# Rings of PSUM banks and SBUF copies for the last thirty groups, without the unread matmuls

## The reference, cut to what matters

```python
offset = _conv(data_im, offset_w)                    # 3x3, 18 channels
mask = jax.nn.sigmoid(_conv(data_im, mask_w))        # 3x3, 9 channels
...
val = w00 * gather(y0i, x0i) + w01 * gather(y0i, x1i) + w10 * gather(y1i, x0i) + w11 * gather(y1i, x1i)
val = val * msk                                      # (B, C, 9 taps, H, W)
out = jnp.einsum('op,bphw->bohw', weight, col)       # (32 x 288) times columns
...
x = x + _L3_conv_ref(_gn(x), ...)
```

## Time and profile before

| what | value |
|---|---|
| median of 3 runs | 1318.24 us (1309.74, 1318.24, 1324.23) |
| the profiled execution | 1326.25 us, its span 1324.4 us |
| TensorE matmuls, weight loads | 748.0 us busy (56%), 335.9 us (25%) |
| VectorE, ScalarE, GpSimd | 667.9 us, 265.7 us, 658.5 us busy |
| mean granted TensorE clock | 0.743 |

### The profile page before, as it was taken

One profiled execution on the slowest core, in us unless ns is written; L12 is line 12 of the kernel. 1 busy time (PEld: TensorE's weight loads), 2 busy tenths in 40 slices (PEclk: granted clock), 3 DMA queues, 4 the chain that ended last, 5 costly groups with the idle time before them and its releaser, 6 DMA issues.

```text
span 1324.4 us, 8552 instructions
## 1 busy us (share of the span) xinstructions
PE 748.0 (56%) x2516; PEld 335.9 (25%) x2517; DVE 667.9 (50%) x913; ACT 265.7 (20%) x360; POOL 658.5 (50%) x619
## 2 busy tenths in 40 slices
PE   3448487777781146465656565500227546655798
PEld 1233132222130123232323223300103212312345
DVE  5988358999672177686777776421003101311230
ACT  1201575555140231121211111100001000100011
POOL 0000006775067736655666635777764757656610
PEclk9669797999795567877677777555657757856799
DMA  4000330000521101111111135211110211111100
GB/s 93 0 0 0 72 80 0 1 0 1 112 68 50 48 23 42 42 40 36 42 42 44 42 77 123 61 52 53 52 48 22 52 38 50 40 40 46 42 12 16
DMA packets 22376, 56.17 MB, mean 42 GB/s; under 512 B 10288, under 2 KB 10672, under 8 KB 21104
## 3 DMA queue, kind: packets, MB, share of 16 engines
q0 software_dynamic: 18432, 37.79, 10.6%
q1 hardware_dynamic: 3056, 15.45, 5.4%
q10 hardware_dynamic: 864, 2.64, 0.9%
HBM read 42.21 MB, written 5.24 MB: 36 GB/s over the span
## 4 chain that ended last, share of the span: by engine, by line
issue 25%; PE 23%; DVE 19%; another core or an unknown queue 15%; ACT 3%; POOL 1%; DMA 1%; DVEq 0%; ACTq 0%; POOLq 0%
PE PS L1389 10%; DVE scratch L1112 4%; PE PS L785 4%; DVE scratch L1038 3%; DVE scratch L1119 2%; PE PS L769 2%; DVE prodg L751 2%; DVE PS L1035 2%; DVE scratch L1043 1%; PE PS L1211 1%; PE PS L852 1%; PE PS L853 1%; PE PS L995 1%; PE PS L787 1%
## 5 line engine op out<-in xcount | busy, mean ns | idle before, releaser
L740 POOL DMA_INDIRECT got<-corner_table,idx_slot x486 | 479.2, 986 | 301.4 <-DVE prodg L751 155.3
L785 PE MATMUL PS<-colT,wt 128*32 128x128 f32 x512 | 93.4, 343 | 216.9 <-issue 163.5
L1389 PE MATMUL PS<-parts,selb 96*128 96x512 bf16 x600 | 168.0, 421 | 77.8 <-issue 76.2
L980 PE MATMUL PS<-parts,selb 96*128 96x512 bf16 (+1 forms) x256 | 87.3, 438 | 121.2 <-DVE scratch L1043 40.6
L759 DVE TENSOR_TENSOR ln_g<-prodg 128x384 f32<-128x384 f32 x51 | 28.5, 559 | 246.1 <-remote 210.3
L1088 POOL TENSOR_TENSOR scratch<-scratch 128x1024 f32<-128x1024 f32 x16 | 37.6, 2350 | 220.3 <-ACT scratch L1070 220.3
L995 PE MATMUL PS<-scratch,wt 128*128 128x512 f32 x256 | 139.7, 673 | 7.7 <-DVE scratch L1043 5.9
L785 PEld LDWEIGHTS PS<-colT,wt 128*32 128x32 f32 x512 | 64.2, 137 | 259.7 <-issue 193.8
L740 POOL DMA_INDIRECT got<-corner_table,idx_all x90 | 88.3, 981 | 65.4 <-DVE prime L1285 38.3
L1389 PEld LDWEIGHTS PS<-parts,selb 96*128 96x128 bf16 x600 | 60.9, 102 | 174.9 <-issue 123.8
L751 DVE TENSOR_TENSOR prodg<-got,coef 128x1152 f32<-128x1152 f32 x64 | 86.9, 1358 | 1.3
(11 more groups left out here) (316 smaller groups left out, 1028.2 us busy)
## 6 DMA issues: line engine op xcount, KB each, us to landing
got<-corner_table,idx_slot POOLq DMA_INDIRECT x486
XN<-ln_g SPq DMA_DIRECT2D x6, 256.0 KB, 5.9
got<-corner_table,idx_all POOLq DMA_INDIRECT x90
corner_table<-scratch SPq DMA_DIRECT2D x1, 1056.0 KB
corner_table<-XN SPq DMA_DIRECT2D x1, 1056.0 KB
X<-in_x SPq DMA_DIRECT2D x4, 256.0 KB, 5.0
corner_table<-scratch SPq DMA_DIRECT2D x1, 992.0 KB
corner_table<-XN SPq DMA_DIRECT2D x1, 992.0 KB
```

The lines of the kernel that those rows point to most:

```text
L740: pool.indirect_dma_start(got[:, slot, tap, :, :].rearrange("p k c -> p (k c)"), None, tables[b], bass.IndirectOffsetOnAxis(ap=index[:, ta ...
L785: nc.tensor.matmul(PS[0:C, 7, 0:P], wt[:, W_L3 + C * r:W_L3 + C * r + C], colT[:, r * P:r * P + P], start=(r == 0), stop=False)
L980: last = nc.tensor.matmul(PS[:, first + n, :], selb[:, which, j, :], parts[:, bass.ds(i * CHUNK + n * BANK, BANK)], start=True, stop=True)
L1389: nc.tensor.matmul(PS[:, n % 4, :], selb[:, 0, 0, :], parts[:, 0:BANK], start=True, stop=True)
```

## The change

1. Signals. `t_psum` and `o_psum` become one semaphore, `turn_done`, raised once a turn by the last instruction of it on TensorE (the last transpose). It is primed with five as `t_psum` was. VectorE waits on it where it waited on `t_psum`; ScalarE waits on it for both copies, so the output copy of a turn too waits for the transposes. This holds from turn 1 on, in the projections and the scan of image 1 too.
2. The loop of turns 34 to 63 is written out on TensorE and ScalarE (`ring_tensor`, `ring_scalar`). Transposes go to banks 0 to 3 in turn, the transpose copies to five places in `scratch`, the products to banks 4, 5 and 7 in turn.
3. Turn G of the ring is the multiplication of group G-4 (not G-2), then the transposes of group G-1. The multiplications of groups 61 and 62 stand in turn 64, and that of 63 behind it with a signal of its own.
4. The 20 unread matmuls of each of the 30 turns are gone.

GpSimd's and SyncE's instructions and VectorE's program stand as they were, but for the semaphore's name.

The diff:

```diff
--- before.py
+++ after.py
@@ -697,7 +697,7 @@
         l3 = {n: sem("l3_" + n) for n in (
             "stats", "totals", "sqrt_go", "sqrt_done", "g_ready", "corner_ready", "right_ready", "shift_done", "below_in", "below_ready", "table_in",
             "zeroed", "g3_in", "g3_ready", "off_psum", "mask_in", "mask_exp", "base_in", "resid_in",
-            "idx_ready", "prod_done", "rows_done", "sum_done", "t_psum", "t_read", "o_psum", "o_read", "out_dma")}
+            "idx_ready", "prod_done", "rows_done", "sum_done", "turn_done", "t_read", "o_read", "out_dma")}
         gathered = [sem(f"gathered{k}") for k in range(SLOTS)]
 
         GLEN = (H + 2) * W
@@ -732,6 +732,8 @@
 
 
 
+
+        REST = GROUPS + 2
 
         def group_gather(pool, b, G, slot, index):
             pool.wait_ge(l3["prod_done"], G + 1)
@@ -755,7 +757,7 @@
             tell(v, nc.vector.tensor_tensor(prodg[:, 6:9, 0:2, :], prodg[:, 6:9, 0:2, :], prodg[:, 6:9, 2:4, :], ALU.add),
                  l3["rows_done"], G + 1)
             colg = colgs[slot]
-            v.wait_ge(l3["t_psum"], G + 1)
+            v.wait_ge(l3["turn_done"], G + 1)
             nc.vector.tensor_tensor(colg[:, 0:3 * P].rearrange("p (t k c) -> p t (k c)", k=2, c=C),
                                     prodg[:, 0:6, 0:2, :].rearrange("p t k c -> p t (k c)"),
                                     prodg[:, 0:6, 2:4, :].rearrange("p t k c -> p t (k c)"), ALU.add)
@@ -767,11 +769,10 @@
             pe.wait_ge(l3["t_read"], G + 1)
             for r in range(4):
                 last = nc.tensor.transpose(PS[:, 6, r * P:r * P + P], colgs[slot][:, r * P:r * P + P], ident)
-            last.then_inc(l3["t_psum"], 1)
+            return last
 
         def group_copy(act, G):
-            act.wait_ge(l3["t_psum"], G + (SLOTS + 1))
-            act.wait_ge(l3["o_psum"], G + 1)
+            act.wait_ge(l3["turn_done"], G + (SLOTS + 1))
             nc.scalar.activation(colT[:, :], PS[:, 6, :], ACT.Copy).then_inc(l3["t_read"], 1)
 
         def group_pixels(t, g):
@@ -784,12 +785,12 @@
             for r in range(4):
                 nc.tensor.matmul(PS[0:C, 7, 0:P], wt[:, W_L3 + C * r:W_L3 + C * r + C], colT[:, r * P:r * P + P],
                                  start=(r == 0), stop=False)
-            nc.tensor.matmul(PS[0:C, 7, 0:P], M(M_IDENT, slice(0, 96), slice(0, C)), group_pixels(G3s[b], g),
-                             start=False, stop=True).then_inc(l3["o_psum"], 1)
+            return nc.tensor.matmul(PS[0:C, 7, 0:P], M(M_IDENT, slice(0, 96), slice(0, C)), group_pixels(G3s[b], g),
+                             start=False, stop=True)
 
         def group_out(act, b, G, g):
 
-            act.wait_ge(l3["o_psum"], G + 2)
+            act.wait_ge(l3["turn_done"], G + (SLOTS + 2))
             act.nop(nofuse=True)
             nc.scalar.activation(group_pixels(G3s[b][0:C, :], g), PS[0:C, 7, 0:P].rearrange("c (q n) -> c q n", q=4),
                                  ACT.Copy).then_inc(l3["o_read"], 1)
@@ -800,13 +801,15 @@
                 b = (G - 2) // GROUPS
                 if (G - 2) % GROUPS == 0:
                     pe.wait_ge(l3["resid_in"], 32 * (b + 1))
-                group_multiply(pe, b, G - 2, G - 2 - b * GROUPS)
+                last = group_multiply(pe, b, G - 2, G - 2 - b * GROUPS)
             if 1 <= G < B * GROUPS + 1:
-                group_transpose(pe, G - 1, (G - 1) % SLOTS)
+                last = group_transpose(pe, G - 1, (G - 1) % SLOTS)
+            if G >= 1:
+                last.then_inc(l3["turn_done"], 1)
 
         def tensor_turn_in_loop(pe, b, G, g, k):
             group_multiply(pe, b, G - 2, g - 2)
-            group_transpose(pe, G - 1, (k - 1) % SLOTS)
+            group_transpose(pe, G - 1, (k - 1) % SLOTS).then_inc(l3["turn_done"], 1)
 
         def scalar_turn(act, G):
             if G >= 2:
@@ -818,6 +821,60 @@
         def scalar_turn_in_loop(act, b, G, g):
             group_out(act, b, G - 2, g - 2)
             group_copy(act, G - 1)
+
+        LAG, FIRST, LAST_GROUP = 4, REST - 1, B * GROUPS - 1
+
+        def ring_psum(G):
+            return PS[:, G % 4, :]
+
+        def ring_colT(G):
+            return scratch[:, G % SLOTS * (4 * P):G % SLOTS * (4 * P) + 4 * P]
+
+        def ring_out(G):
+            return PS[0:C, (4, 5, 7)[G % 3], 0:P]
+
+        def ring_transpose(pe, G):
+            pe.wait_ge(l3["sum_done"], G + 1)
+            pe.wait_ge(l3["t_read"], max(G - 4, FIRST - 1) + 2)
+            for r in range(4):
+                last = nc.tensor.transpose(ring_psum(G)[:, r * P:r * P + P], colgs[G % SLOTS][:, r * P:r * P + P], ident)
+            return last
+
+        def ring_multiply(pe, G):
+            pe.wait_ge(l3["t_read"], G + 2)
+            pe.wait_ge(l3["o_read"], max(G - 3, FIRST - 1) + 2)
+            for r in range(4):
+                nc.tensor.matmul(ring_out(G), wt[:, W_L3 + C * r:W_L3 + C * r + C], ring_colT(G)[:, r * P:r * P + P],
+                                 start=(r == 0), stop=False)
+            return nc.tensor.matmul(ring_out(G), M(M_IDENT, slice(0, 96), slice(0, C)), group_pixels(G3s[1], G - GROUPS),
+                                    start=False, stop=True)
+
+        def ring_tensor(pe):
+            group_multiply(pe, 1, FIRST - 1, FIRST - 1 - GROUPS)
+            for G in range(REST, LAST_GROUP + 2):
+                if G - LAG >= FIRST:
+                    ring_multiply(pe, G - LAG)
+                if G == LAST_GROUP + 1:
+                    for k in range(G - LAG + 1, LAST_GROUP):
+                        ring_multiply(pe, k)
+                ring_transpose(pe, G - 1).then_inc(l3["turn_done"], 1)
+            ring_multiply(pe, LAST_GROUP).then_inc(l3["turn_done"], 1)
+
+        def ring_drain(act, G, turn):
+            act.wait_ge(l3["turn_done"], turn + SLOTS)
+            nc.scalar.activation(group_pixels(G3s[1][0:C, :], G - GROUPS), ring_out(G).rearrange("c (q n) -> c q n", q=4),
+                                 ACT.Copy).then_inc(l3["o_read"], 1)
+
+        def ring_scalar(act):
+            group_out(act, 1, FIRST - 1, FIRST - 1 - GROUPS)
+            for G in range(REST, LAST_GROUP + 2):
+                if G - LAG >= FIRST:
+                    ring_drain(act, G - LAG, G)
+                act.wait_ge(l3["turn_done"], G + SLOTS)
+                nc.scalar.activation(ring_colT(G - 1), ring_psum(G - 1), ACT.Copy).then_inc(l3["t_read"], 1)
+            for k in range(LAST_GROUP + 2 - LAG, LAST_GROUP):
+                ring_drain(act, k, LAST_GROUP + 1)
+            ring_drain(act, LAST_GROUP, LAST_GROUP + 2)
 
         def vector_turn(v, G):
             if G < B * GROUPS:
@@ -1315,7 +1372,6 @@
         TURNS = len(TURN_AFTER)
         IN_SCAN = 4
         IN_PREPARE = IN_SCAN + NCHUNK * TURNS
-        REST = GROUPS + 2
         assert TURNS == SLOTS and (B * GROUPS - REST) % SLOTS == 0
         EARLY = 28
 
@@ -1382,13 +1438,7 @@
                 pe.wait_ge(l3["resid_in"], 32 * B)
                 pe.wait_ge(l3["below_in"], 4 * B)
                 pe.wait_ge(l3["below_ready"], 4 * B)
-                with nc.tensor.Fori(0, (B * GROUPS - REST) // SLOTS) as i:
-                    for k in range(SLOTS):
-                        tensor_turn_in_loop(pe, 1, i * SLOTS + (REST + k), i * SLOTS + (REST - GROUPS + k), REST + k)
-                        for n in range(20):
-                            nc.tensor.matmul(PS[:, n % 4, :], selb[:, 0, 0, :], parts[:, 0:BANK], start=True, stop=True)
-                for G in range(B * GROUPS, B * GROUPS + 2):
-                    tensor_turn(pe, G)
+                ring_tensor(pe)
 
             @block.scalar
             def _(act):
@@ -1405,11 +1455,7 @@
                 prep[1][2](act, lambda k: scalar_turn(act, IN_PREPARE + k))
                 for G in range(IN_PREPARE + 3, REST):
                     scalar_turn(act, G)
-                with nc.scalar.Fori(0, (B * GROUPS - REST) // SLOTS) as i:
-                    for k in range(SLOTS):
-                        scalar_turn_in_loop(act, 1, i * SLOTS + (REST + k), i * SLOTS + (REST - GROUPS + k))
-                scalar_turn(act, B * GROUPS)
-                scalar_turn(act, B * GROUPS + 1)
+                ring_scalar(act)
 
             @block.vector
             def _(v):
@@ -1418,7 +1464,7 @@
                 for k, (signal, n) in enumerate((
                         (sc["h_done"], 2), (sc["hc_done"], 1), (sc["y_done"], 2), (sc["y_used"], 1), (sc["b_used"], 1),
                         (sc["dbu_done"], 2),
-                        (l3["prod_done"], SLOTS), (l3["t_psum"], SLOTS), (l3["t_read"], 1), (l3["o_psum"], 1), (l3["o_read"], 1))):
+                        (l3["prod_done"], SLOTS), (l3["turn_done"], SLOTS), (l3["t_read"], 1), (l3["o_read"], 1))):
                     nc.vector.memset(prime[:, k:k + 1], 0.0).then_inc(signal, n)
                 vchain(v, nc.vector.memset(carry[:, :], 0.0))
                 project_vector(v, 0)
```

## The result

| | before | changed |
|---|---|---|
| median | 1320.92 us (4 runs, 1309.74 to 1324.23) | 1262.63 us (4 runs, 1258.07 to 1272.08) |
| profiled execution, its span | 1326.25, 1324.4 us | 1260.2, 1258.4 us |
| mean granted TensorE clock | 0.743 | 0.704 |

The ratio is 0.9581, 95% interval 0.9534 to 0.9628: 4.2% faster. I had forecast 1267 us, inside 1226 to 1308. A repeat later gave 0.9544 (0.9478 to 0.961).

What follows compares the result with a forecast made beforehand. GpSimd's gathers, held by late TensorE signals, bound the kernel: 1207 us unheld plus 28 pauses, 33 tail, 2.7 output and 2 signals gave a 1273 us span, 1275 profiled, less 8 for the median: 1267 us, range 1226 to 1308.

Steps and rivals of the forecast that it cites:

- What bounds the kernel: Layer 3: GpSimd paces at 11.5 us a group, held by TensorE signals late 1.37 us per instruction while gathers run.
- The unread matmuls: Turns 34 to 63: removing them saves 4.48 us of each 6.1 us clear turn, leaving 3.4 us, and 55 us clogged.
- The ring's start: Turns 35 and 36, transposes alone at 11 us each, free slots early; GpSimd's first pause moves from 989 to 1012 us.
- The pauses: GpSimd's waits from 989 us on: 28 us, half of 57, so GpSimd ends at 1235 us instead of 1264.
- The tail: After GpSimd's end, six groups behind at 3.4 us a turn: 33 us, then 2.7 us of output.
- The signals: ScalarE's output copy now waits for the transposes in turns 1 to 33: 2 us of cost, bounds 0 and 15.
- alarm: Start of the changed profile: the sum is wrong if anything ahead of 930 us moved by over 5 us.
- A (no pauses): Ring turns: lateness is a hidden delay or the store never fills; GpSimd ends at 1207, time 1224 us; 20%.
- B (the tail alone): Only the tail after GpSimd's end gets shorter; pauses stay 57 us, time 1301 us; 14%.
- C (short windows): Ring: GpSimd restarts at one free slot, clear windows stay short, 17 us a turn, slower at 1346 us; 8%.
- D (no gain): Whole kernel: TensorE's instructions don't count, pauses grow by what the tail loses, 1318 us; 6%.

Runs made afterwards that it cites:

- e11: The changed kernel with two of the four weight products of each ring group left out, in a clogged session: 1257.97 us, ratio 0.952 to before.
- e8: The kernel before without its 600 unread matmuls, all else as it was, in a clogged session: 1281.1 us, ratio 0.9648 to before.
- e10: The changed kernel with twenty unread matmuls put back into each ring turn, in a clogged session: 1318.37 us, ratio 1.0012 to before.
- e1: The kernel before without its 600 unread matmuls, all else as it was, in a quiet session: 1135.36 us, ratio 0.9985 to before.
- e6: The kernel before with seventy unread matmuls of 64 columns per loop turn instead of twenty of 512, clogged session: 1331.14 us, ratio 1.0068.
- e7: The changed kernel as it is, measured again in a clogged session: 1267.31 us, ratio 0.9544 to before.
- e3: The kernel before with only its two signals of a turn merged into one, in a quiet session: 1135.87 us, ratio 0.9984.
- e4: The changed kernel with two of the four weight products of each ring group left out, in a quiet session: 1135.12 us, ratio 0.9985.
- e2: The changed kernel with twenty unread matmuls put back into each ring turn, in a quiet session: 1135.18 us, ratio 0.9977 to before.

## Why the prediction held, point by point

**What bounds the kernel** was right for a clogged session. GpSimd's 11.5 us a group is the pace and late TensorE signals hold it; turns of 28 instructions are 39 us in the changed kernel too. That lateness goes by instructions (each matmul counted with its load) and is no fixed delay is shown by e11.

**The unread matmuls** carried the forecast and carry the result: e8, which only drops them, gives 0.9648, where the whole change gives 0.9544 beside it and 0.9581 in the first measurement. Their price in the tail was right (4.48 us a turn, e10). For what is left of a turn I took 3.4 us; e8 has 4.2 us at half clock, and the ring 1.8 at the full one: behind the last gather the granted clock comes back to 2.4 GHz in both, without filler. That the clock is lost elsewhere costs nothing: e1 runs TensorE at 0.50 and equals before in a quiet session, because TensorE waits for GpSimd's groups anyway:

```profile
860.00:930.00 70.00, 21.26 (x87) 14.40 (x88) 15.55 (x30) 5.19 (x12) 53.55 (x55) 0.50 0.19 52
934.00:1130.00 196.00, 58.73 (x238) 39.30 (x238) 44.13 (x85) 14.67 (x34) 142.72 (x146) 0.50 0.20 52
```

**The ring's start** is the step that failed. I had the signals of turns 34 to 36 at 969, 980 and 991 us and GpSimd running on to 1012 us. GpSimd stopped at 965.5 us, after 13 groups where before's run had 14, and turn 34's signal came at 976.24, in the pause. The next two, at 981.88 and 984.75, were passed in clear time, so the eight-instruction turns never stood in a clogged stretch and released nothing early. Before's 989 us, from which I reckoned, was itself the exception: in the six other clogged traces, with two signals (e8, e6) as with one, GpSimd's first pause comes after 12 or 13 groups, never after 14. What the ring gives instead is back-to-back turns where TensorE is clear: 24.8 us from the last gather to the end in e7 and 31.2 in the first measurement, 37.5 in e8. In the medians that is 14 us, with intervals that overlap, and with filler it is nothing (e10). The Trainium skill, "TensorE: Matmul & The Clock Gate", HAM oscillation, reports no further gain from PSUM double-buffering; e10 and all quiet sessions agree with it, e7 against e8 leans the other way and does not settle it.

**The pauses** were 31.1 us where I took 28, the middle of a range of 0 to 57. The size came out near, the course did not: I had at most one pause more after the first, and there were two, at 1113.71 and 1135.43 us, one group apart. That 28 and 31 are close is in part luck. **The tail** behind GpSimd's end was 30.3 us where I took 35.7: turns at 1.8 us and not 3.4. **The signals** I gave 2 us of cost; e3 finds none (0.9984) in a quiet session. I had set as an alarm that nothing ahead of 930 us may move by over 5 us, and the first gather of image 1 came 12.6 us earlier. But over the clogged executions it lies at 826.4, 836.5 and 839.7 us with two signals and at 827.1, 830.6, 833.3 and 834.6 with one. The two sets overlap (means 834.2 and 831.4), so the 12.6 us may well be chance of the profiled execution; whether the merged signal gives a few microseconds in a clogged session was not measured alone. On the profiled scale the forecast of 1273 us of span was 15 us too high: 12.6 of it is this start, 7 the tail and the signals, against 5 us more in the pauses and around them.

**The rivals.** A (no pauses) fell: three pauses. B (the tail alone) fell: 423.4 us of gathers became 400.1. C (short windows) fell as a whole: 8 to 9 turns passed in the clear time around the first and the third pause. At the second it was right: only one turn's signal (1110.66 us) came, TensorE was not yet clear when GpSimd began again, and after one group it stopped again. D (no gain) fell in clogged sessions. The range that I gave, from 1226 us, leaves out A's own 1224.

What no case held is that a quiet session exists. There the parts of the change are worth some 0.2% (e1 to e4), since TensorE's turns lie beside GpSimd's groups; for the whole change this is inferred, not measured. The forecast was of the size of a disturbance that the trace of before showed, and that it came true is luck in this: the comparison fell into a clogged session. Why a session clogs stays open. It is not the chip by its number, nor the kernel's instructions, and the gathers alone don't do it: the DMA share from 860 to 930 us is 0.19 in e1 and in before alike. Whether something else at work on the machine does it, no run tells.

## What to carry to other kernels

When an engine is late though its own work is short, count its instructions in the late stretch and divide: a constant per instruction says to remove instructions, not to add buffers. Filler that keeps a clock up was paid here where its engine is the path, above all in the tail, and was worth nothing while that engine waited for another. And before a wait is priced, take the same kernel in another session: here one number was 1137 and 1320 us, and most of the gain lived in the difference.

## What the runs showed of the hardware

- In a clogged session TensorE's signals come late once a stretch of indirect gathers has run for a while. Settled, a turn costs 1.37 us for each TensorE instruction, loads counted (28 in 38.5 us, 20 in 27.6, the mean of five turns), though its matmuls may long have been executed (2.5 us of work, the signal 79 us behind, in e11). On the way there TensorE goes in steps of 0.7 us with several instructions in each (e6).
- It ends some 4 to 5 us into a pause of GpSimd: matmuls 2.8 us apart come 0.7 us apart from 1128.85 us on in the changed kernel, where GpSimd had stopped at 1124.65, and back to back from 1083.66 us on in before, where it had stopped at 1079.39. The changed kernel's pause of 6.5 us before 1113.71 did not end it: from 1116.26 us on the matmuls came 2.1 to 2.8 us apart again.
- The same kernel before, with the same inputs, ran in 1137 to 1139 us in four sessions and in 1319 to 1323 in three. e2's kernel, traced in both kinds, shows no wait of GpSimd for VectorE over image 1 in the quiet one and 45.2 us in the clogged. No run here tells the cause.
- Up to the first gather of image 0 the two kinds are alike (364.65 to 368.86 us). Clogged, 77 to 85 us are lost from there to image 1's first gather (e2, e4 and e1 against their repeats). The change touches this stretch only by its merged signal, whose worth there was not measured alone.
